# A two-layer mixture of experts: second expert layer in 39 slots of 128 rows instead of 23 of 256

## What is computed

```
logits = x_flat @ router_w.T + router_b          # 8 experts
topk_prob, topk_idx = jax.lax.top_k(softmax(logits), 2)
for e in range(8):
    gate = jnp.sum(jnp.where(topk_idx == e, topk_prob, 0.0), axis=-1)
    h = jax.nn.gelu(x_flat @ w1[e].T + b1[e])    # 256 -> 1024
    y = y + gate[:, None] * (h @ w2[e].T + b2[e])  # 1024 -> 256
```

## Time and profile before

| what | us |
|---|---|
| three runs, median (lowest to highest) | 822.8 (820.49 to 828.12) |
| the profiled execution, its own time | 825.46 |
| span of its instructions | 823.6 |
| slot stage of layer 1, first up matmul to last down matmul | 539.1 to 796.9 |
| after it (scatter, read back, add, store) | 796.9 to 823.6 |

### The profile page before, as it was taken

How to read it: one execution, slowest core, us unless ns; L and a number is a source line. 1 busy time by engine, 2 the same in 40 slices (tenths; PEclk the granted TensorE clock), 3 DMA queues, 4 the chain that set the end, 5 groups by cost and what they waited for, 6 DMA issues and landing times.

```text
span 823.6 us, 16877 instructions
## 1 busy us (share of the span) xinstructions
PE 609.0 (74%) x5984; PEld 535.8 (65%) x5984; DVE 550.1 (67%) x975; ACT 379.6 (46%) x568; POOL 436.4 (53%) x406
## 2 busy tenths in 40 slices
PE   5957899999996407676634552079999999999960
PEld 4646888888985306565523442059999899999850
DVE  3953699999988576767646877836554554555536
ACT  2644267777764424555414676114444333333420
POOL 6663668898886147767328863443333333332120
PEclk9987699999998758999985776579999999999995
DMA  8200002221122315768742322021111111121018
GB/s 278 74 4 27 26 2 66 65 65 42 57 66 71 90 68 175 214 204 237 191 144 85 98 72 78 13 64 36 43 53 53 53 53 49 44 51 35 21 40 305
DMA packets 35824, 70.27 MB, mean 85 GB/s; under 512 B 5985, under 2 KB 22114, under 8 KB 35490
## 3 DMA queue, kind: packets, MB, share of 16 engines
q1 hardware_dynamic: 25442, 42.70, 16.5%
q0 software_dynamic: 8160, 22.29, 9.7%
q10 hardware_dynamic: 2144, 4.19, 1.4%
HBM read 50.81 MB, written 18.35 MB: 84 GB/s over the span
## 4 chain that ended last, share of the span: by engine, by line
PE 44%; DVE 22%; issue 10%; POOL 7%; ACT 7%; DMA 6%; DVEq 1%; SPq 1%; POOLq 0%; ACTq 0%; another core or an unknown queue 0%
PE banks L1183 42%; DMA sorted_y<-slot_region 3%; POOL wb_region L549 2%; PE banks L1381 1%; DVE x_res L1110 1%; DVE w_region L876 1%; DVE rs L868 1%; DVE w_region L881 1%; ACT w_region L656 1%; DMA w_region<-token_y 1%; POOL rv L457 1%; DVE slot_region L1080 1%; ACT w_region L589 1%; DVE w_region L1015 1%; DVE slot_region L1015 1%
## 5 line engine op out<-in xcount | busy, mean ns | idle before, releaser
L1183 PE MATMUL banks<-w_region 128*128 128x128 f16 (+5 forms) x1948 | 174.2, 251 | 31.9 <-POOL w_region L508 12.1
L1183 PEld LDWEIGHTS banks<-w_region 128*128 128x128 f16 (+1 forms) x1948 | 160.0, 125 | 41.5 <-POOL w_region L508 12.4
L1183 PE MATMUL banks<-w_region,wb_region 128*128 (+1 forms) x1168 | 137.6, 277 | 11.8 <-DMA wb_region<-wk 7.2
L1183 PEld LDWEIGHTS banks<-w_region,wb_region 128*128 128x128 f16 (+1 forms) x1168 | 119.1, 105 | 25.8 <-issue 8.5
L559 POOL DMA_INDIRECT token_y<-slot_region,lg x46 | 45.4, 987 | 164.9 <-DVE slot_region L1080 157.9
L1183 PE MATMUL banks<-slot_region,w_region 128*128 128x256 f16 x1104 | 127.1, 275 | 2.8 <-issue 2.8
L718 ACT ACTIVATE wb_region<-wb_region 128x1024 f32<-128x1024 f32 x46 | 48.6, 1057 | 171.4 <-DVE wb_region L1062 147.2
L1183 PEld LDWEIGHTS banks<-slot_region,w_region 128*128 x1104 | 107.8, 99 | 16.8 <-issue 3.9
L1062 DVE SCALAR_TENSOR_TENSOR wb_region<-banks,b_s 128x1024 f32<-128x1024 f32 x46 | 56.1, 1224 | 85.3 <-PE banks L1183 54.3
L517 POOL DMA_INDIRECT slot_region<-normed_rows,index x92 | 94.4, 1026 | 34.2 <-issue 24.4
L1183 PE MATMUL banks<-wb_region,w_region 128*128 (+1 forms) x344 | 55.4, 311 | 37.3 <-DVE slot_region L1080 25.0
(11 more groups left out here) (233 smaller groups left out, 1072.6 us busy)
## 6 DMA issues: line engine op xcount, KB each, us to landing
staging<-w_t SPq DMA_DIRECT2D x32, 512.0 KB
sorted_y<-slot_region SPq DMA_DIRECT2D x23, 256.0 KB
x_res<-x SPq DMA_DIRECT2D x4, 512.0 KB, 9.3
staging<-w_in SPq DMA_DIRECT2D x4, 512.0 KB
normed_rows<-w_region SPq DMA_DIRECT2D x16, 128.0 KB, 1.7
staging<-w_out SPq DMA_DIRECT2D x4, 512.0 KB
normed_rows<-wb_region SPq DMA_DIRECT2D x16, 128.0 KB
w_region<-token_y ACTq DMA_DIRECT2D x2, 1024.0 KB, 8.7
```

The costliest lines, as they stand in the source:

```text
L1183: return t.matmul(o, a, b, start=start, stop=stop)
```

## The change

Layer 0 keeps 23 slots of 256 rows, and its instructions stand in the same order as before; several semaphores now serve both layers (`made` adds the first layer's count). For layer 1:

- Slots have one tile of 128 rows: NSLOTS[1] = (4096 + 8 x 127) // 128 = 39. RING, AHEAD and the number of `y` buffers YB are now 8, 4 and 4 (counted in slots).
- `slot_up_last` reads its stationary weights from a fixed place, `w_slot`, which lies in the staging buffers (free by then). DVE copies the slot's expert's 128x4096 f16 input weights there, `slot_weights`, in two halves of 128x4x512. The copy of half a for slot j waits until PE has finished half a of slot j-1's up (`half_up`), and PE's half waits for the copy.
- One bias, one gelu, one high part and one low part per slot, each still 128x1024, since all 8 chunks of 128 rows now fit in the two banks. Columns are 128x512, the output row block is 128x256, and there is one gather and one scatter a slot.
- The DVE order of a step s is: register load for slot s+1, both weight copies for slot s+1, bias of slot s, out of slot s-3, low of slot s-1, columns of slot s+1. PE's order of a step is: transposes of slot s, up of slot s-1, down of slot s-3.
- `expert` lies in a tile `heads` that the attention part used.

```diff
-    A = 2
-    SW = A * P
-    NSLOT = (2 * T + E * (SW - 1)) // SW
+    TILES = (2, 1)
+    NSLOTS = [(2 * T + E * (a * P - 1)) // (a * P) for a in TILES]
+    LAG = 2
...
+            m.RING, m.AHEAD, m.YB = 8 // m.A, 4 // m.A, 4 // m.A
...
+        w_slot = STG[:, :, :].rearrange("p a b -> p (a b)").bitcast(F16).rearrange("p (s n) -> p s n", n=H1)
...
+            def slot_weights(j, a):
+
+                m = moes[1]
+                if j >= 1:
+                    dve.wait_ge(sem("half_up"), 2 * (j - 1) + a + 1)
+                half = slice(a * m.H // 2, (a + 1) * m.H // 2)
+                src = m.wa[:, bass.ds(expert_of[j] * (2 * DC * m.H), 2 * DC * m.H)].rearrange("p (s n) -> p s n", n=m.H)
+                v.tensor_copy(w_slot[:, :, half], src[:, :, half]).then_inc(sem("slot_weights"), 1)
...
+            def slots_of_last():
...
+                n = NSLOTS[1]
+                for s in range(-1, n + LAG + 1):
+                    if s + 1 < n:
+                        expert_at(s + 1)
+                        for a in range(2):
+                            slot_weights(s + 1, a)
+                        if s == -1:
+                            slot_cols(1, 0)
+                    if 0 <= s < n:
+                        slot_bias(1, s)
+                    if 0 <= s - LAG - 1 < n:
+                        slot_out(1, s - LAG - 1)
+                    if 0 <= s - 1 < n:
+                        slot_lo(1, s - 1)
+                    if 0 <= s + 1 < n and s >= 0:
+                        slot_cols(1, s + 1)
...
+            def slot_up_last(j):
+
+                m = moes[1]
+                pe.wait_ge(sem("slot_cols"), made(1, j + 1))
+                if j >= 2:
+                    pe.wait_ge(sem("h_biased"), made(1, j - 1))
+                xT, ps = m.xT[:, j % 2], hidden(m, j)
+                for a in range(2):
+                    pe.wait_ge(sem("slot_weights"), 2 * j + a + 1)
+                    for hc in range(a * m.HC // 2, (a + 1) * m.HC // 2):
+                        w = slice(hc * P, (hc + 1) * P)
+                        for dc in range(DC):
+                            last = three(ps[:, hc, :], w_slot[:, dc, w], w_slot[:, DC + dc, w],
+                                         xT[:, dc, :], xT[:, DC + dc, :], dc == 0, dc == DC - 1)
+                    last.then_inc(sem("half_up"), 1)
```

More of the change, by code:

```diff
@@ L512, in gather_rows @@
                 m = moes[layer]
-                for a in range(A):
-                    if j >= RING:
-                        pool.wait_ge(sem(f"slot_tr{layer}"), j - RING + 1)
-                    q = A * j + a
+                for a in range(m.A):
+                    if j >= m.RING:
+                        pool.wait_ge(sem("slot_tr"), made(layer, j - m.RING + 1))
+                    q = m.A * j + a
                     g.indirect_dma_start(
-                        out=m.rows[:, j % RING, a, :], out_offset=None, in_=rows_dram,
+                        out=m.rows[:, j % m.RING, a, :], out_offset=None, in_=rows_dram,
                         in_offset=bass.IndirectOffsetOnAxis(ap=index[:, q:q + 1], axis=0)).then_inc(
-                        sem(f"rows_gathered{layer}_{j % RING}"), 16)
+                        gathered(layer, j)[0], 16)
             def slot_rows(layer):
@@ L526, in slot_rows @@
                     pool.wait_ge(sem(f"rows_kept{1 + 2 * layer}_{b}"), 16 * (NT // 2))
-                for j in range(AHEAD):
+                m = moes[layer]
+                for j in range(m.AHEAD):
                     gather_rows(layer, j)
@@ L530, in slot_rows @@
                     pool.wait_ge(sem("back_ready"), 1)
-                for j in range(NSLOT + 3 * layer):
-                    if j + AHEAD < NSLOT:
-                        gather_rows(layer, j + AHEAD)
+                for j in range(m.NSLOT + 3 * layer):
+                    if j + m.AHEAD < m.NSLOT:
+                        gather_rows(layer, j + m.AHEAD)
                     if layer == 1 and j >= 3:
@@ L939, in route @@
                 r = routes[layer]
+                SW, NQ, NSLOT = moes[layer].SW, NQS[layer], NSLOTS[layer]
                 def cut(n):
@@ new lines, in slot_bias @@
+            def slot_bias(layer, j):
+                m = moes[layer]
+                dve.wait_ge(*up_done(layer, j + 1))
+                if j >= 2:
+                    dve.wait_ge(sem("h_lo"), made(layer, j - 1))
+                bias = m.b[:, bass.ds(expert_of[j] * m.HC, m.HC)]
+                v.scalar_tensor_tensor(out=m.g[:, j % 2], in0=hidden(m, j), scalar=1.0 / WS,
+                                       in1=bias[:, :, None].to_broadcast([P, m.HC, m.SW]),
+                                       op0=ALU.mult, op1=ALU.add).then_inc(sem("h_biased"), 1)
@@ L1101, in slots_of @@
                     k = PRE + A_CH + s
-                    if layer == 0 and k < NCH - LATE and k % 2:
+                    if k < NCH - LATE and k % 2:
                         split_lo(k)
+            def slots_of_last():
+                dve.wait_ge(sem("b1_loaded"), 16)
+                dve.wait_ge(sem("b2_loaded1"), 16)
+                for b in range(2):
+                    dve.wait_ge(sem(f"chunk_lo{b}"), NCH // 2)
+                n = NSLOTS[1]
[10 more added lines that the diff above has]
+                        slot_out(1, s - LAG - 1)
+                    if 0 <= s - 1 < n:
+                        slot_lo(1, s - 1)
+                    if 0 <= s + 1 < n and s >= 0:
+                        slot_cols(1, s + 1)
@@ L1374, in slot_tr @@
                 m = moes[layer]
-                pe.wait_ge(sem(f"rows_gathered{layer}_{j % RING}"), 16 * A * (j // RING + 1))
+                pe.wait_ge(*gathered(layer, j))
                 if j >= 2:
-                    pe.wait_ge(sem(f"slot_cols{layer}"), j - 1)
-                cols = slot_columns(j)
-                for a in range(A):
+                    pe.wait_ge(sem("slot_cols"), made(layer, j - 1))
+                cols = slot_columns(m, j)
+                for a in range(m.A):
                     for c in range(2 * DC):
-                        last = t.transpose(cols[:, c, a * P:(a + 1) * P], m.rows[:, j % RING, a, c * P:(c + 1) * P],
+                        last = t.transpose(cols[:, c, a * P:(a + 1) * P], m.rows[:, j % m.RING, a, c * P:(c + 1) * P],
```

270 lines of the change are left out of this document (130 added, 140 removed).

## The result

The changed kernel takes 832.87 us (median of 4, 831.84 to 833.66), the kernel before 823.97 (median of 4, 820.49 to 828.12) beside it: a ratio of 1.0095, 95% interval 1.0068 to 1.0122. It is slower by 8.9 us, 1%, and the interval leaves out 1. The forecast was slower, by 15.9.

What follows compares the result with a forecast made beforehand. PE bounds the kernel now; DVE's row behind each up would bound the changed one. Layer 1: 263.0 + 10.7 + 4 = 277.7 against 257.8, +19.9; with -2.5 and -1.5, +15.9: 839 us, range 824 to 862.

Steps and rivals of the forecast that it cites:

- DVE's row of five: Layer 1, between ups: second weight copy, bias, out, low and columns run in a row on DVE; chance 0.62.
- period: Layer 1, from one up to the next: 6.92 us a slot, PE working 5.5 and waiting 1.4.
- lost at the start: Start of layer 1's slots, an up at half clock among it: 4 us taken, against 5.1 before.
- last slot: Layer 1 after 38 periods: up, bias, ACT, low, hand-over and last down, 10.7 us.
- stage: Layer 1's slots, first up to last down: 277.7 us against 257.8 before, +19.9.
- hand-over from DVE to PE: Layer 1, from DVE's end to PE's first matmul: 0.25 us a slot.
- (1) PE stays the bound: Layer 1: DVE's five steps and two hand-overs fit behind PE's other work; 53 us less, 786; chance 0.05.
- (2) Shorter hand-overs: Layer 1: hand-overs shorter than in layer 0; periods of 6.4 to 6.7 give 819 to 830 us; chance 0.14.
- (3) A copy with one saving: Layer 1's weight copy gets one saving only: 859 us; with neither, 932; together chance 0.07.
- (4) POOL holds up the copies: Layer 1: POOL's scatter and gather delay the weight copies; up to 37 us, 859 to 876; chance 0.06.
- (5) The clock falls in the gaps: Layer 1: PE's clock drops in the new gaps; with one slot in five so, +32 us, 871; chance 0.04.
- (6) A slower pace of narrow matmuls: Layer 1: 128-column matmuls keep 0.08 us rather than 0.056 over long runs; 885 us at most; chance 0.02.

Runs made afterwards that it cites:

- e11: The changed kernel, unchanged, measured and profiled a second time: 837.57 us against 828.22 for the kernel before, ratio 1.0106.
- experiment 6: The changed kernel without weight copies, its up reading weights through the register: 870.74 us in the changed order, 843.77 us with the columns copied first.
- experiment 1: The changed kernel with the columns copy moved from the end to the front of DVE's step: 786.04 us against 827.63, ratio 0.9489.

## Why the prediction came out as it did

The forecast was slower, by DVE's row of five behind each up, and that is what happened; the size was 16 us where 9 were measured. The 832.87 lies near the lower edge of the forecast's own range, 831 to 848, and its period, 6.68, just below the 6.7 to 7.1 from which that range was made; it is 1.9 us above what the prediction would have called no change. In the prediction's terms, against the two profiles of the changed kernel:

| term | forecast | after | e11 |
|---|---|---|---|
| period | 6.92 | 6.68 | 6.68 |
| 38 periods | 263.0 | 253.8 | 253.8 |
| lost at the start | 4 | 0.2 | 6.2 |
| last slot | 10.7 | 11.25 | 11.25 |
| stage | 277.7 | 265.3 | 271.3 |
| earlier start of the stage | -2.5 | -3.3 | -2.4 |
| after the stage | -1.5 | -1.2 | -1.4 |

(The last two lines are against the first profile of before, 114.0 and 26.7.)

- **The mis-sized term is the hand-over from DVE to PE.** It was 0.25 us, from the earlier trace rows; it measured 646.43 - 646.37 = 0.06. That row is of a down of layer 0, whose first matmul has its weights addressed through a register. Here the up's first matmul has a fixed address. Where the up was given the register back (experiment 6), the hand-over was 644.91 - (644.36 + 0.42) = 0.13, so the addressing is a part of it, and not all. This is 0.19 of the 0.24 us a slot, 38 x 0.19 = 7.2 of the 9.2 us in the periods. The other 0.05 came from bias, out and low, counted 1.14, 0.35 and 1.15, measured 1.13, 0.33 and 1.13.
- **The other terms of the period held**: up 2.85, PE to DVE 0.15, copy 0.61 (0.69 long, taken from two savings that each had a row), columns 0.42. The transposes and the down lie in the row's shadow.
- **The start loss** of 4 lay between the two profiles, whose mean is 3.2. It was taken from the first up of the kernel before; what it stands for here, copies behind POOL's gathers and a clock that falls again in the gaps, the sum did not have. That the number is near is luck.
- **The last slot** was 0.55 longer: the last 48 matmuls, 5.43 us, are the downs of two slots, and they started 799.20 - 793.38 = 5.82 after the last up, when a low had ended. The forecast had the first of the two out of the way by then.
- **The sum.** With the means of the profiles, layer 1's slots are 10.4 us longer, the stretch ahead of them 3.2 shorter, the end 1.5 shorter: +5.7. Layer 0's slots were 2.3 longer in these profiles, which lies within the spread of the kernel before alone. Together +8.0, against 8.9 and 9.3 measured.

The rivals. (1) PE stays the bound: wrong for the changed kernel, and right once the columns are copied first, since nothing then stands between them and the up. Its time, 786 us, was met too, though from 832.9 that is 47 us and not the 53 of its working, and by another way: the five steps did not shrink, they left the path. (2) Shorter hand-overs: right as to the mechanism, with a period of 6.68 at the upper edge of its 6.4 to 6.7, which alone makes 839 - 9 = 830 us; the median is 3 above that, no more than start and layer 0's slots vary. Forecast and rival met between them. (3) A copy with one saving: no, 0.69. (4) POOL holds up the copies: not in the steady slots of the changed kernel, where the second copy is 0.15 behind the up in every one. But it came near. The scatter's issue grew to 1.7 us beside the low, and the gather ended at 641.49, 0.08 after the first copy had started. With the out moved it did happen, in 31 slots at 0.60, 19 us, and 842.66 - 822.54 = 20 us by the medians, the small end of the 20 to 37 that it was given. And it is seen at the start of e11. (5) The clock falls in the gaps: not in the steady slots, 1.00 over 180 us with a gap of 0.98 in each; at the start yes, to 0.50 after gaps of 3.27 and 3.97 us, where the up behind took 1.4 and 2.5 us more. (6) A slower pace of narrow matmuls: no. In experiment 1 a stream of 48 + 24 + 4 matmuls every 5.52 us leaves 0.056 us for one of 128 columns over 1872 of them; the sustained 81 ns of the Trainium skill (TensorE: Matmul & The Clock Gate, Back-to-back issue gap) are not seen here.

## What to carry to other kernels

When an engine hands work on within a loop, list what stands ahead of the instruction that the bound engine waits for, and put that instruction first; the same work cost 47 us more in the wrong order than in the right one. Take a hand-over from a row whose consumer has the same form of address, since a term of 0.2 us counts once a slot. Before an instruction on one engine is moved, look which transfers start behind it: the out, moved out of the path, dragged POOL's pair onto the weight copies and cost more than it saved. And look at the first turns of a loop by themselves: here they held waits and a low clock that the steady turns do not have.

## What was not expected of the hardware

- Register rows between matmuls cost nothing at 256 columns and some 0.045 us each at 128 (4.35 us for an up instead of 2.85).
- A gather of 0.97 us that starts 1.84 us after the up, behind a scatter, delays VectorE's passing of a wait on PE by 0.58 us, without lengthening the copy; at 0.78 us after the up, or without the gather, there is no such delay. Where the copy had started 0.27 us before the gather (experiment 1), the copies were on time and the gather's issue grew to 1.26 us. Why is open.
- The scatter's issue took 1.68 us on average beside the low, against the 0.97 of the earlier trace rows; it harmed nothing, since POOL was idle for 156.6 / 39 = 4.0 us ahead of each.
- Two executions of one program can differ by 6 us in the first four slots: by whether VectorE's first copy starts between POOL's eight gathers or only behind them all, and by the clock, which was at 0.50 again after PE had been idle for 3.27 us in one execution and 3.97 in the other.
